# Third convolution: the weighing matmuls of a chunk in one run, small matmuls behind the gathers, and a quarter of its edge sends issued in the first convolution's loop

## The reference

```python
def spline_conv(x, row, col, basis, idx, W, b):
    z = jnp.einsum('ni,kio->nko', x, W).reshape(N * K, Fout)
    gathered = z[col[:, None] * K + idx]
    msg = jnp.einsum('es,eso->eo', basis, gathered)
    out = jax.ops.segment_sum(msg, row, num_segments=N)
    deg = jax.ops.segment_sum(jnp.ones_like(msg[:, 0]), row, num_segments=N)
    return out / jnp.maximum(deg, 1.0)[:, None] + b
...
basis, idx = spline_basis(pseudo)
h = jnp.ones((N, 1), x.dtype)
h = jax.nn.elu(spline_conv(h, row, col, basis, idx, stn1_w, stn1_b))
h = jax.nn.elu(spline_conv(h, row, col, basis, idx, stn2_w, stn2_b))
h = jax.nn.elu(h @ stn3_w + stn3_b)
t = h @ stn4_w + stn4_b
new_pseudo = jnp.clip(pseudo + t[col] - t[row], 0.0, 1.0)
basis2, idx2 = spline_basis(new_pseudo)
return spline_conv(x, row, col, basis2, idx2, conv_w, conv_b)
```

## Time and profile before

| | |
|---|---|
| median of 3 runs | 10374.85 us (10366.98 to 10381.05) |
| the profiled execution's own time | 10362.97 us |
| its span in the profile | 10361.0 us |
| first convolution, both of its blocks | about 2596 to 3229 us of the span |
| third convolution | about 6400 to 8415 us of the span |
| busy over the whole span | PE 71%, DVE 73%, ACT 45%, POOL 57% |

### The profile page before, as it was taken

One profiled execution on the slowest core, in us unless ns is written; L12 is line 12 of the kernel. 1 busy time (PEld: TensorE's weight loads), 2 busy tenths in 40 slices (PEclk: granted clock), 3 DMA queues, 4 the chain that ended last, 5 costly groups with the idle time before them and its releaser, 6 DMA issues. The chain is left out here.

```text
span 10361.0 us, 393328 instructions
## 1 busy us (share of the span) xinstructions
PE 7407.7 (71%) x147710; PEld 6528.2 (63%) x147711; DVE 7530.9 (73%) x18535; ACT 4644.2 (45%) x12114; POOL 5944.5 (57%) x5974
## 2 busy tenths in 40 slices
PE   5465555554773656565658995899999978888888
PEld 4455555554563555555557884777777757777776
DVE  7688888886774444445456883888888869999887
ACT  0011111110552333333335662444454459999997
POOL 0477777776334777777776770777777731111111
PEclk6555555555555878787879996999999989989888
DMA  1222233332102333333333221222222225555554
GB/s 45 36 82 74 74 74 76 74 75 49 25 8 67 112 114 108 115 111 116 114 110 96 75 76 27 62 63 62 63 63 61 63 67 142 142 142 142 140 139 99
DMA packets 850875, 875.93 MB, mean 85 GB/s; under 512 B 629325, under 2 KB 632837, under 8 KB 850286
## 3 DMA queue, kind: packets, MB, share of 16 engines
q1 hardware_dynamic: 623150, 526.57, 18.4%
q0 software_dynamic: 227648, 348.32, 13.1%
HBM read 631.28 MB, written 135.27 MB: 74 GB/s over the span
## 5 line engine op out<-in xcount | busy, mean ns | idle before, releaser
L1573 ACT ACTIVATE c_products<-c_pa 125x512 f32<-125x512 f32 x2368 | 1222.7, 603 | 1786.1 <-PE c_pa L1617 1770.2
L1448 POOL DMA_INDIRECT c_near_ranked<-h_rows,c_idx x1568 | 1656.4, 1056 | 477.7 <-issue 477.4
L786 POOL DMA_INDIRECT edges_by_rank<-rank_stage,rank_idx x1568 | 1607.1, 1025 | 502.7 <-issue 466.4
L1900 POOL DMA_INDIRECT edges_b<-c_send_rows,c_send_idx x1184 | 1316.6, 1112 | 397.4 <-issue 357.5
L1617 PE MATMUL c_pa<-c_near_apart,c_basis 32*125 32x128 f32 x18944 | 743.5, 294 | 1006.3 <-DVE c_near_apart L1536 904.3
L1617 PEld LDWEIGHTS c_pa<-c_near_apart,c_basis 32*125 32x125 f32 x18944 | 636.6, 195 | 1124.9 <-issue 1124.9
L1628 PE MATMUL c_py<-c_products,c_weights 125*64 125x128 f32 x18944 | 1212.4, 283 | 0.0
L2413 POOL DMA_DIRECT2D rows<-local_rows x548 | 294.7, 538 | 1586.1 <-DVE hot_d L2431 1438.4
L295 PE MATMUL acc_s<-hot_col,hot_row 128*123 128x91 f16 x3136 | 421.2, 312 | 990.7 <-ACT start_table L741 795.8
L1628 PEld LDWEIGHTS c_py<-c_products,c_weights 125*64 125x64 f32 x18944 | 1069.0, 141 | 58.0 <-issue 0.2
L2059 ACT ACTIVATE c_products<-c_pa 125x256 f32<-125x256 f32 x2368 | 710.8, 384 | 787.7 <-PE c_pa L2142 787.7
(11 more groups left out here) (410 smaller groups left out, 18864.6 us busy)
## 6 DMA issues: line engine op xcount, KB each, us to landing
rows<-local_rows POOLq DMA_DIRECT2D x548, 256.0 KB, 4.0
own_d<-hparts SPq DMA_DIRECT2D x2192, 48.0 KB, 3.0
hi_rows_in<-hi_rows SPq DMA_DIRECT2D x392, 256.0 KB
c_dst_rows_in<-dst_rows SPq DMA_DIRECT2D x148, 512.0 KB
near_by_rank<-c_near_ranked SPq DMA_DIRECT2D x98, 768.0 KB, 5.0
rows_both<-hi_rows SPq DMA_DIRECT2D x196, 196.0 KB
near_h<-c_near_h SPq DMA_DIRECT2D x74, 512.0 KB
c_near<-near_h SPq DMA_DIRECT2D x148, 256.0 KB
```

The source lines that it names most:

```text
L786: pool.indirect_dma_start(g.ranked, bass.IndirectOffsetOnAxis(idx[:, r, q:q + 1], 0), stage[:, r, q, :], None, bounds_check=last_rank, oob ...
L1448: pool.indirect_dma_start(near[:, b, q, :], None, g.h1_rows, bass.IndirectOffsetOnAxis(idx[:, b, q:q + 1], 0), bounds_check=last_node, oob ...
L1573: last = act.activation(by_round[:, half, r, rnd], pa[0:K3, r, 0:TR * P].rearrange("p (f e) -> p f e", f=width), ACT.Copy)
L1900: pool.indirect_dma_start(g.edges_b, bass.IndirectOffsetOnAxis(sending.idx[:, n, q:q + 1], 0), sending.rows[:, n, q, :], None, bounds_chec ...
```

## The change

In the first convolution's loop, GpSimd issues the sends of the last 37 steps (159 to 195; `FIRST` is 37): after every fetch of two gathers come half a step's sends (4 indirect DMAs), and after the loop the 8 of the last step. SP loads their rows and indices: the first four steps ahead of everything else in the block, the others in a loop after its other work. In the third convolution every fourth chunk sends nothing, on GpSimd and on SP.

In the third convolution's chunk, PE does `gather` directly behind the outer products of its round, `fold_out` and `node_sums` behind the gather, all 32 matmuls of `weigh` between the outer products and the gather of round 3, and `spread` at the end of the chunk. DVE does `take_own` after `choose` 3 instead of after `choose` 2.

```diff
+FIRST = (STEPS - EARLY) // DEEP
 (first_conv)
             def _(sp):
+                for r in range(DEEP):
+                    bring_edges(SENT + r, r)
                 sp.wait_ge(s_set, 1)
...
                 sp.wait_ge(s_idx_put, 16)
+                with sp.Fori(1, FIRST // DEEP) as i:
+                    for r in range(DEEP):
+                        sp.wait_ge(sending.s_sent[r], i * (STEP * 16) + 16)
+                        bring_edges(i * DEEP + (SENT + r), r)
...
             def _(pool):
+                g.open_sent(pool, sending.s_sent)
+                def send_edges(i, r, part):
+                    if part == 0:
+                        pool.wait_ge(sending.s_in[r], i * 32 + 32)
+                    pool.sem_inc(sending.s_tick, 1)
+                    for q in range(part * (STEP // 2), (part + 1) * (STEP // 2)):
+                        pool.indirect_dma_start(g.edges_b, bass.IndirectOffsetOnAxis(sending.idx[:, r, q:q + 1], 0),
+                                                sending.rows[:, r, q, :], None, bounds_check=last_place,
+                                                oob_is_err=False).then_inc(sending.s_sent[r], 16)
...
+                def fetch_and_send(i, r):
+                    for part in range(2):
+                        fetch(i * (2 * DEEP) + (r * 2 + part + 2))
+                        send_edges(i, r, part)
+
-                for m in range(4):
+                for m in range(2):
                     fetch(m)
+                fetch_and_send(0, 0)
                 pool.wait_ge(s_ranks, 16)
                 pool.tensor_copy(ranks_out[:, :, :], ranks_in[:, :, :, 3]).then_inc(s_cast, 1)
-                with pool.Fori(4, NPAIRS) as m:
-                    fetch(m)
+                for r in range(1, DEEP):
+                    fetch_and_send(0, r)
+                with pool.Fori(1, FIRST // DEEP) as i:
+                    for r in range(DEEP):
+                        fetch_and_send(i, r)
+                for r in range(FIRST % DEEP):
+                    for part in range(2):
+                        send_edges(FIRST // DEEP, r, part)
 (third_conv, GpSimd; SP alike)
+                    if n == DEEP - 1:
+                        continue
                     pool.wait_ge(sending.s_in[n], i * 32 + 32)
 (third_conv, DVE)
                     choose(k + 3, 1 - half, 2)
-                    take_own(k + 3)
                 if left >= 2:
                     make_basis(k + 2, half, i + 2, 1)
                 if left >= 3:
                     choose(k + 3, 1 - half, 3)
+                    take_own(k + 3)
                     move(k + 3, 1 - half)
 (third_conv, PE)
                 for rnd in range(ROUNDS):
                     if left >= 1:
                         outer_products(k + 1, 1 - half, rnd)
+                    if rnd == ROUNDS - 1:
+                        weigh(k, half)
+                    if left >= 3:
+                        gather(k + 3, 1 - half, rnd)
                     if rnd == 0 and not first:
                         fold_out(k - 1, k + 4 if left >= 2 else NCK + 1)
                     if rnd == 1 and not first:
                         node_sums(k - 1)
-                    weigh(k, half, rnd)
-                    if left >= 3:
-                        gather(k + 3, 1 - half, rnd)
-                        if rnd == 2:
-                            spread(k + 3)
+                    if rnd == ROUNDS - 1 and left >= 3:
+                        spread(k + 3)
```

More of the change, by code:

```diff
@@ L1055, in _, with bring_edges @@
             def _(sp):
+                def bring_edges(step, r):
+                    sp.dma_start(sending.rows[:, r, :, :],
+                                 edge_rows[:, ds(step * STEP, STEP), :]).then_inc(sending.s_in[r], 16)
+                    sp.dma_start(sending.idx[:, r, :], edge_idx[:, ds(step * STEP, STEP)]).then_inc(sending.s_in[r], 16)
+                for r in range(DEEP):
+                    bring_edges(SENT + r, r)
                 sp.wait_ge(s_set, 1)
@@ L1902, in _ @@
                                                 oob_is_err=False).then_inc(sending.s_sent[n], 16)
-            for n in range(DEEP):
+            for n in range(DEEP - 1):
                 pool.wait_ge(sending.s_sent[n], NCK // DEEP * (STEP * 16) + 16)
@@ L2147, in outer_products, with weigh @@
                 last.then_inc(s_outer, 1)
[L2149 to L2153 removed]
+            def weigh(k, half):
+                pe.wait_ge(s_kept, k * ROUNDS + (ROUNDS + 1))
+                pe.sem_inc(s_pe_turn, 1)
+                for f in range(F):
                     n = f % KP
```

30 lines of the change are left out of this document (19 added, 11 removed).

## The result

The changed kernel takes 10424.51 us (median of 6 runs, 10421.77 to 10428.99), the kernel before 10372.34 us (6 runs on the same chip, 10366.98 to 10381.05). The ratio is 1.005, with a 95% interval of 1.0039 to 1.006: 52 us slower. The profiled execution took 10422.69 us, its span is 10421.0 us.

What follows compares the result with a forecast made beforehand. The prediction saw no full engine in the first convolution and a DVE-PE ring setting the third's 13.08 us chunk. Its terms, +87 + 4 - 2 - 37 = +52 us, on 10374.85 gave 10427 us, range 10350 to 10485.

Steps and rivals of the forecast that it cites:

- +87: First convolution: four sends a pair make POOL the bound, 9.0 us a pair instead of 7.78; ends +44 and +151.
- +4: First convolution: last sends beside DVE's last two pairs, 0 to 5 us; opening DMAs and loads, 0 to 5 us once.
- the fetch part: First convolution: POOL's index copy and two gathers for a pair, 3.76 us before, taken as 3.6 with the change.
- -37: Third convolution: the new PE and DVE order cuts 142 chunks from 13.08 to 12.82 us; ends -82 and +31.
- -2: Third convolution's start: with fewer sends, the own shift of a later chunk comes sooner, saving 2 us.
- The ring: Third convolution: choose 3, move, hats, round 2 and 3 outer products, whole weighing and round 3 gather set 12.82 us a chunk.
- POOL waits for DVE there: Third convolution: expected sign that POOL, with fewer sends, would wait for DVE; no size given.
- The prediction's 13.03 us for POOL: Third convolution: POOL's group rows summed per chunk before the change, read as POOL never resting; 1.8 us wait for DVE.
- Rival 1: Third convolution: POOL held it and now comes free, chunk 12.14 us, -133 us there, 10331 us total; chance 0.12.
- Rival 2: Third convolution: the ring over ACT does not close, DVE's 12.5 us set the chunk, 10382 us total; chance 0.13.
- Rival 3: First convolution: the sends hide, POOL busy 513 of 619 us, 10338 us total; chance 0.04.
- Rival 4: Third convolution slower too: weighing keeps 2.28 us, PE loses 0.1, ring 13.3 us, 10495 us total; chance 0.13.

Runs made afterwards that it cites:

- the kernel with only the spread late: The change with weighing in quarters again, spread still at the chunk's end, own take behind choose 3: 1.0 of the kernel before, +5 us.
- the early copy: The kernel with only the spread late, with POOL's next index copy moved behind this pair's gathers, two index buffers: 0.9929 of the kernel before, -75 us.
- The kernel with an eighth moved and the copy on DVE: The kernel with only the spread late, but an eighth of the sends moved and DVE doing the first convolution's index copy: 0.9928 of the kernel before.
- the copy on POOL: The kernel with only the spread late, but an eighth of the sends moved instead of a quarter: 0.9934 of the kernel before, -71 us.
- the one with the spread late and all sends: The kernel before with the spread late and weighing in quarters, all eight sends in every third-convolution chunk: 1.0018 of the kernel before, +21 us.

## Why the prediction was right

Forecast +52, measured +52; range and direction held. The agreement to the microsecond is luck: the first convolution cost 17 us more than the sum had, the third's loop 16 less, its end 7 more, which no term had, and the profiled execution of the kernel before lay 9 us under its median.

**First convolution, +87 and +4 predicted, +108 measured.** The mechanism held: POOL had 4.0 us to spare and got more, its waiting disappeared, DVE now waits 1.7 us a pair for the gathers' transfers, and copies stand one behind the other. The size failed in the step "the fetch part ... I take 3.6 as that place moves". In the pair shown the four sends cost 5.15 us instead of 5.44, but the fetch 4.16 instead of 3.6: the wait for DVE's product moved from the second gather (1.43 to 1.01 us) to the copy, with all its length (0.19 to 0.83). The 1.43 had been read as something that a new place does away with. DVE waits for POOL's gathers once a pair; the two stayed in phase for 53 pairs, and the same instruction was hit in each of them. Where the copy then missed the product, a pair took 8.95 us, the forecast's 9.0.

**The rule weighed there.** The prediction set the rule of the Trainium skill ("SBUF — State Buffer", section "Who interferes with whom") aside, since by it alone several sends of a pair would be held up. That section has a DVE instruction with two inputs in SBUF contend with a GpSimd instruction that reads SBUF. The runs bear this out for this product: 0.83 us for a copy that starts with it, 0.39 for one that starts halfway. What was wrong is how it was applied: not every send is exposed, only one that stands at certain places against the product (the table above), and in the changed kernel between 2700 and 3100 us none does; the copy does. Where that section gives it as inferred that such a product does not hold up the making of descriptors, this case differs: indirect DMAs that started 0.22 to 0.34 us into it took 1.37 to 1.48 us against 0.97 to 1.19 clear of it.

**Third convolution, -37 and -2 predicted, -55 measured in the loop and +7 behind it.** The ring was named step for step, and it is what sets the chunk: 12.70 us against 12.82. Weight loads of 1.69 us and 1.89 to the gather are what was worked out. The 0.12 us are `choose` 3 (0.52 instead of 0.60, since `take_own` fits into the gap behind it), the gather (1.05 for 1.08) and `TENSOR_REDUCE` to `move` (2.70 for 2.72). Over 142 chunks that is 17 us. The 7 us come after the last `own_wide`. The end grew by 4 us with the new order alone and not at all with the weighing in quarters, so it comes with the weighing in one run or the place of the small matmuls, for which the sum had no term there. One sign was off: "POOL waits for DVE there". POOL waits 1.9 us a chunk, and the profile puts it down to the load of the sends' indices.

The prediction's 13.03 us for POOL is busy plus idle time over a window, without the row of the index copy; with it the sum is the chunk itself, as it is for any engine. What it rightly showed is that almost none of the idle time was a wait.

**"By itself this saves nothing there; it takes away the danger that POOL (13.03 us a chunk) holds a faster loop."** Both halves are shown: the sends alone bring nothing in the third convolution's loop (+3 us), the order alone +9, the two together -55.

**The rivals.** Rival 1 fell: without any sends the chunk is 12.95 us, not 12.14. The unrolled start was no measure of the loop. Rival 2's bound of 12.5 us exists, 12.41 in the kernel with the ring open, but the change did not reach it. Rival 3 fell: by busy time alone it would have stood, 508 of 714 us, but POOL's idle time was gaps between its own instructions. It holds at half the sends, where two fit into a pair. Rival 4's extra 0.1 us in the weighing did not show.

## What to carry to other kernels

Slack that is to take in moved work is counted in the helper engine's own row, with the gap between its instructions: 4.0 us a pair held two sends of 1.3 to 1.7 us, and not four. Where two limits lie within 1% of each other (here the ring and POOL), an edit against one shows nothing until the other is lifted, so such edits are tried in a square of four and not one by one; and work taken from a queue is taken evenly from each turn, not as one turn in eight. When the order on an engine is changed to take out a wait, the wait is moved with the smallest edit that does it: here, with POOL relieved, the spread's place gained 0.70 us a chunk (13.11 to 12.41), and the run of weighing and the small matmuls' place that came with it gave 0.29 back, and 7.7 us at the end of the stage.

## What was not expected of the hardware

DVE's product of two tiles (0.82 us) holds an instruction of POOL by where the two stand, and not only one that starts inside it: copies that started 0.01 to 0.04 us ahead of it took 0.87 to 0.89 us where a clear one takes 0.19. The loss is therefore a matter of phase: 0.64 us or none for the same copy, and it can lie on another instruction after any edit.

It goes the other way too. The third convolution's chunk differs with code that is the same: 12.41 us with the copy of the first convolution where the change has it, 12.24 where it is early or on DVE. That is 26 us of the 75 or so that the early copy brought. DVE's waits hardly tell the two apart; the length of one instruction does, in the kernel with only the spread late and in the one with the early copy (6700 to 8200 us):
```profile
L2074 DVE TENSOR_SCALAR c_node_hot<-iotaf,node_in_chunk x120: 350/549/637, 6711.6 to 8188.0; 128x256 f32<-128x256 f32 x120
```
```profile
L2081 DVE TENSOR_SCALAR c_node_hot<-iotaf,node_in_chunk x122: 350/351/566, 6707.3 to 8188.7; 128x256 f32<-128x256 f32 x122
```
The averages are 0.49 and 0.38 us, 0.12 of the 0.17 us in a chunk. In the first kernel 74 of the 120 start 0.48 to 0.58 us behind the start of an indirect DMA of POOL; they last 0.54 to 0.64 us and end 0.09 to 0.12 us behind that DMA. The others, at most 0.37 us behind such a start or clear of POOL, last 0.35 to 0.41. In the second only 15 stand in the bad place. So a DVE instruction, too, pays by where it meets POOL. The kernel with an eighth moved and the copy on DVE has none in the bad place: 0.35 us against 0.47 with the copy on POOL, and a chunk of 12.56 us against 12.63. What sets this phase from one kernel to the next stays open.

TensorE's granted clock in the first convolution was 0.50 (1.2 GHz) in most profiles and 1.00 (2.4 GHz) in those of the kernel without the third's sends and of the one with the spread late and all sends. The whole stage took 572.0 and 571.7 us there, against 571.2 and 571.6 at 0.50, so the stage does not hang on it. What decided the level no run here shows.
